# A Mamba block and a routed expert layer on one core: the norm of the block behind moved one step, and the order of the tail on VectorE and GpSimd

## The reference, cut to what matters

```python
def step(h, inp):                     # Mamba: 512 channels, 16 states, over 1024 tokens
    xt, dt_t, B_t, C_t = inp
    A_disc = jnp.exp(A[None, None, :] * dt_t[:, :, None])
    h = A_disc * h + dt_t[:, :, None] * B_t[:, None, :] * xt[:, :, None]
    y_t = jnp.einsum('bed,bd->be', h, C_t) + D * xt
    return (h, y_t)
...
y = jax.nn.silu(y + res)
return y @ W_out.T
...
x = _layernorm(x + mamba(x), axis=-1)                 # (x - m) / sqrt(v + 1e-5)
router_probs = jax.nn.softmax(x @ router_w.T)
expert_weights, expert_idx = jax.lax.top_k(router_probs, 2)
# each of the two experts: gelu(x @ w1.T + b1) @ w2.T + b2, weighted and summed
x = _layernorm(x + moe(x), axis=-1)
```

## Time and profile before

| | us |
|---|---|
| median of 3 runs | 1429.03 (1427.63 to 1429.11) |
| the profiled execution, own time | 1429.47 |
| its span in the profile | 1427.7 |
| PE busy | 1288.1 (90%) |
| DVE busy | 1104.4 (77%) |
| POOL busy | 1052.6 (74%) |
| ACT busy | 993.4 (70%) |
| first scan to last scan (`mamba`'s blocks) | 40.4 to 855.1 |
| mean granted clock of PE | 0.962 of full speed |

### The profile page before, as it was taken

How to read it: one execution, slowest core, us unless ns; L and a number is a source line. 1 busy time by engine, 2 the same in 40 slices (tenths; PEclk the granted TensorE clock), 3 DMA queues, 4 the chain that set the end, 5 groups by cost and what they waited for, 6 DMA issues and landing times. The chain is left out here.

```text
span 1427.7 us, 28835 instructions
## 1 busy us (share of the span) xinstructions
PE 1288.1 (90%) x8807; PEld 1090.3 (76%) x8808; DVE 1104.4 (77%) x1836; ACT 993.4 (70%) x1364; POOL 1052.6 (74%) x920
## 2 busy tenths in 40 slices
PE   6799899999998998998997996499999999999991
PEld 2468687787777787877886885499999999999981
DVE  6879999899899899899898896665665665665554
ACT  6899998999988999988988963334433433433434
POOL 3589798798998989998989997455555555555544
PEclk8799999999999999999999998699999999999995
DMA  8523141132331332331322327424465723522216
GB/s 280 173 79 97 61 122 63 56 120 79 101 108 68 99 103 71 105 104 64 109 82 75 111 85 246 152 42 107 123 160 144 206 41 74 140 41 37 34 20 243
DMA packets 91017, 150.75 MB, mean 106 GB/s; under 512 B 10892, under 2 KB 43276, under 8 KB 90928
## 3 DMA queue, kind: packets, MB, share of 16 engines
q1 hardware_dynamic: 73216, 121.24, 26.4%
q0 software_dynamic: 16704, 27.29, 9.5%
q10 hardware_dynamic: 1008, 1.07, 0.3%
HBM read 100.79 MB, written 48.78 MB: 105 GB/s over the span
## 5 line engine op out<-in xcount | busy, mean ns | idle before, releaser
L1448 POOL TENSOR_TENSOR arena<-arena 128x1024 f32<-128x1024 f32 x252 | 598.5, 2388 | 16.5 <-DVE arena L1107 10.1
L492 PE MATMUL d_ps<-ident,arena 128*128 128x128 f32 x2048 | 320.7, 280 | 44.2 <-DVE arena L1107 36.7
L492 PEld LDWEIGHTS d_ps<-ident,arena 128*128 128x128 f32 x2048 | 240.9, 143 | 150.4 <-DVE arena L1107 73.1
L1107 DVE TENSOR_TENSOR_SCAN arena<-arena,carry,d_ps 128x512 f32<-128x512 f32 x256 | 314.5, 1264 | 28.5 <-PE d_ps L492 21.5
L793 ACT ACTIVATE arena<-u_tok,b_tok 128x512 f32<-128x512 f32 x508 | 324.5, 711 | 6.5 <-PE d_ps L492 5.1
L1107 DVE TENSOR_TENSOR_SCAN arena<-arena,d_ps 128x512 f32<-128x512 f32 x256 | 301.2, 1207 | 30.1 <-PE d_ps L492 19.7
L505 PE MATMUL y_ps<-ident,arena 128*128 128x128 f32 x2048 | 297.3, 274 | 6.8 <-POOL arena L1448 5.5
L1796 ACT ACTIVATE h_t<-ht_ps 128x512 f32<-128x512 f32 x142 | 84.4, 594 | 284.0 <-PE ht_ps L1851 284.0
L807 ACT ACTIVATE arena<-dt,neg_a 128x2048 f32<-128x2048 f32 x127 | 253.1, 1993 | 2.3 <-DVE arena L1107 2.1
L505 PEld LDWEIGHTS y_ps<-ident,arena 128*128 128x128 f32 x2048 | 238.0, 142 | 9.5 <-POOL arena L1448 6.6
L1836 PE MATMUL h_ps<-arena,xg_t 128*128 x852 | 218.1, 405 | 1.3 <-DVE xg_t L1928 1.3
(11 more groups left out here) (230 smaller groups left out, 1552.7 us busy)
## 6 DMA issues: line engine op xcount, KB each, us to landing
arena<-c_rows SPq DMA_DIRECT2D x128, 256.0 KB, 3.3
arena<-weight_parts SPq DMA_DIRECT2D x20, 1024.0 KB, 5.5
weight_parts<-arena SPq DMA_DIRECT2D x64, 256.0 KB, 3.6
xg<-expert_rows POOLq DMA_DIRECT2D x71, 130.0 KB, 2.4
arena<-in_pieces SPq DMA_DIRECT2D x16, 512.0 KB, 8.9
arena<-in_pieces SPq DMA_DIRECT2D x64, 128.0 KB, 3.3
expert_out<-arena SPq DMA_DIRECT2D x1, 4224.0 KB, 15.2
weight_parts<-arena SPq DMA_DIRECT2D x4, 1024.0 KB, 4.6
```

Of the source, the lines that this page charges most:

```text
L492: last = nc.tensor.matmul(d_ps[:, c % 2, j * P:(j + 1) * P], ub[:, g % U_RING, j, c * P:(c + 1) * P], t.ident[:], start=True, stop=True, i ...
L1107: nc.vector.tensor_tensor_scan(h[:, g % H_RING, c, :], decay[:, g % D_RING, c, :], d_ps[:, c % 2, :], 0.0 if i % 2 == 0 else carry[:, n, c ...
L1448: nc.gpsimd.tensor_tensor(h[:, g % H_RING, lo:hi, :], h[:, g % H_RING, lo:hi, :], c_row[:, g % C_RING:g % C_RING + 1, :].broadcast_to([P, ...
```

## The change

Three edits, all of order. No instruction, DMA, buffer or semaphore is added or taken away, and the counts that are waited for stay the same.

1. ACT: `normed()` at the end of step 13 instead of step 14, in blocks 1 to 6. It now comes behind `ut_out(0)` and before `ut_out(1)`. In block 7 it stays at step 12.
2. DVE, in the tail: `copy_group(2)` is ahead of `router_place()` instead of behind it and behind a low part. `own_low(0)` and `own_low(1)` stand together behind the last `norm_group`, ahead of `router_pick(r)`. `own_low(2)`, `(3)` and `(4)`, which stood in the tail, move behind `tables()`, ahead of the seven that were there, so that ten stand there.
3. POOL, in the tail: before, the order was send 0, root 0, send 1, root 1, send 2, root 2, send 3, root 3, sends 4 to 7 (of block 6). Now it is send 0, root 0, send 1, root 1, root 2, root 3, sends 2 to 7.

```diff
--- before.py
+++ after.py
@@ -1074,7 +1074,7 @@
                         xp_out(e, 1)
                     if front and n == 13:
                         ut_out(0)
-                    if back and n == (12 if i == BLOCKS - 1 else 14):
+                    if back and n == (12 if i == BLOCKS - 1 else 13):
                         normed()
             iterations(act, step)
             store_tails(act, range(EXPERTS // 2, EXPERTS))
@@ -1279,9 +1279,8 @@
                     router_sum()
                     router_invert()
                     router_rank()
+                    copy_group(2)
                     router_place()
-                    own_low(0)
-                    copy_group(2)
                     add_group(0)
                     copy_group(3)
                     add_group(1)
@@ -1291,11 +1290,9 @@
                     add_group(3)
                     norm_group(2)
                     norm_group(3)
+                    own_low(0)
                     own_low(1)
-                    own_low(2)
                     router_pick(r)
-                    own_low(3)
-                    own_low(4)
                     router_sum(r)
                     router_invert(r)
                     router_rank(r)
@@ -1426,7 +1423,7 @@
             nc.vector.memset(member[:, TT, :], 0.0)
             iterations(dve, step)
             tables()
-            for m in range(5, W_RING * W_LOADS):
+            for m in range(2, W_RING * W_LOADS):
                 own_low(m)
 
         @block.gpsimd
@@ -1569,10 +1566,11 @@
                                                         (tail_i, [[REGION, EXPERTS]], 0, 0), (pad_i, [[0, 1]], TOKENS, 1)):
                         nc.gpsimd.iota(out, pattern=pattern, base=base, channel_multiplier=channel).then_inc(made, 1)
                     send_rows(p, 0)
-                    for j in range(TT):
+                    rstd_group(0)
+                    send_rows(p, 1)
+                    for j in range(1, TT):
                         rstd_group(j)
-                        send_rows(p, j + 1)
-                    for m in range(TT + 1, TT * TOPK):
+                    for m in range(2, TT * TOPK):
                         send_rows(p, m)
                     router_member(r)
                     router_shift(r)
```

## The result

The changed kernel takes 1415.34 us (median of 4 runs, 1412.16 to 1415.51) against 1429.07 us for the kernel before in the same session. The ratio is 0.9897, with a 95% interval of 0.9878 to 0.9916. The profiled execution is the fastest of the four: 1412.16 us, with a span of 1410.5.

The account below looks back on a forecast made before the run. Bound: across block ends ACT, DVE and PE wait in turn, while ACT work could fill ACT's earlier idle time. Five blocks at 1.45 us, plus 0 for the sixth and the tail, give 7.25: 1429.03 becomes 1421.8, range 1418.0 to 1426.0.

Parts of the forecast that it names:

- Part 1: Blocks 1 to 6: ACT's norm a step sooner, in ACT's idle time; 7.25 us sooner, bounds 4.7 and 9.2.
- the sum of 7.25: Block ends: five blocks at 1.45 us each plus 0 for the sixth block.
- Odd blocks: Ends of blocks 1, 3 and 5: norm fits ACT's idle 2.21; 1.45 us gained each, bounds 1.2 and 1.84.
- the decay's wait: Block after an odd block: DVE's 2.12 us wait for ACT's decay stays, both being ahead by the same.
- from there PE ran to the end of the next block's first transposes in 2.55: Odd block's end: PE's transposes start 1.2 us sooner, then take 2.55 as before, ending at 245.35.
- Rival A: Block ends: ACT is all of the chain, five blocks give 1.84 us each, 9.2, so 1419.8; chance 0.17.
- Even blocks: Ends of blocks 2 and 4: 1.45 us each, bounds 1.0 and 1.6; POOL's products leave 1.57 of slack.
- Block 6: Its end: gain 0; DVE scans delayed up to 1.0 us in step 14 lie under a 3.31 wait; otherwise 0.9 paid.
- Part 2: Tail reordered on POOL and DVE: last norm 1.95 us sooner, net 0; bounds 0.9 sooner and 1.2 later.
- a sign of being wrong: Tail: the prediction would be wrong if POOL's sends or the first x part moved by more than 1 us.
- one such: Tail: one of six sends held 0.9 us by the second low part; `router_member(r)` at about 885.8 instead of 885.27.
- the loads of rows: Tail: POOL's first loads now run beside low parts; one took 0.61 us there before, so no cost taken.

Follow-up runs that it names:

- experiment 1: Norm moved to step 13 in odd blocks alone, old tail, against the kernel before: 1424.12 against 1429.14 us.
- experiment 2: Norm moved to step 13 in blocks 2, 4 and 6 alone, old tail, against the kernel before: 1421.89 us, ratio 0.9952.
- experiment 3: Kernel before, norm and tail unmoved, DVE's dt-xc multiplies asked for at other scans in odd blocks: 1427.35 against 1429.14 us.
- experiment 4: Changed kernel with DVE's first dt-xc multiply one scan earlier in blocks 3 and 5: 1418.21 against 1414.58 us for the changed kernel.
- Experiment 6: Kernel before with two of the norm's four instructions in step 13, two in step 14, blocks 1 to 6: 1422.82 against 1428.59 us.
- experiment 8: Changed kernel with the norm back in step 14, so the new tail alone, against the kernel before: 1428.22 against 1429.14 us.

## Why the prediction was wrong

**The step that failed: Part 1 takes the middle of a block as fixed.** The text says "all of the PE-full middle starts 1.45 sooner", and the sum of 7.25 has no term for it. It rests on one middle, that of block 2, where PE has no gap. In block 3 PE was busy 23.62 of 25 us. In blocks 3 and 5 the middle held 2.4 and 2.1 us in which DVE's multiply waited for POOL, and the change took them away by shifting DVE against POOL at the even blocks' ends: by 1.4 us in block 3, and by 1.8 in block 5, where the scans come 8.2 sooner and POOL's last products of block 4 6.4. Experiments 1, 2, 3 and 4 show it from four sides: without the shift there is no gain, with it there is, by moving the multiply the gain comes without the norm, and by moving it back it goes. This is 4.5 of the 6.5 us missed; the ends were 0.95 too small in the sum and the tail 0.9.

**Odd blocks: mechanism right, size too small.** The norm went into ACT's idle time as said, the tap came 1.85 sooner (forecast 1.8), the decay's wait stayed. 1.45 was forecast, 1.7 to 1.8 measured. The mis-sized term is "from there PE ran to the end of the next block's first transposes in 2.55": it takes 245.65 - 243.31 = 2.34 now that DVE's scans are sooner; and the transposes start 1.35 sooner, not 1.2. Experiment 6 adds that of a shift of 1.03 on ACT 0.97 to 0.98 comes through, so for the odd blocks Rival A, that the chain is ACT's, was the better account.

**Even blocks: right.** 1.35 and 1.65 against 1.45 (bounds 1.0 and 1.6), with POOL as the bound that was named: the sums now start 0.10 after the products. Block 4's 1.65 lies a hair above its bound. That the norms overrun ACT's idle time does not show in these numbers. But this is also where the shift comes from, since DVE gains there and POOL does not. **Block 6: right.** In step 14 DVE falls back by 0.66, less than the 1.0 allowed for, and block 7 gives it back.

**Part 2, the tail: 0 forecast, 0.8 to 0.9 by medians, 1.4 in the profiles.** Neither median is clear of the noise. The first x part came 1.4 sooner against the last scan, more than the 1 us that the prediction had named as a sign of being wrong. The last norm came 1.9 sooner, as forecast, and the six sends started where they were said to. The wrong term is the "one such" send that is held (0.9) and with it the half us of delay. The second send started at 865.77, as the first low part ended and 0.01 us ahead of the second; it kept its 0.97. In all six profiles with both new orders it did, but nothing in the change was made to bring that about: the order was decided by a hair. The low parts after the tables cost nothing, and the loads of rows beside them took 0.6, as the prediction had it.

**Profiles and medians.** The profiled execution of before lost 1.26 us to the low clock in block 7, and the one of after had the best mean clock of its four (0.968 against 0.963 to 0.964), so the profiles differ by 17.2 us and the medians by 13.7. The parts add up to the latter, 8.2 + 4.5 + 0.9 = 13.6, with the tail's 0.9 as the least certain of them.

**How the hold works.** Over the 14 profiles with this multiply, in all 123 cases where it was asked for more than 0.2 us before the end of a POOL tensor_tensor under way, its length was that remainder plus 1.08 us (1.077 to 1.088). So it did not go on before POOL's instruction was over. When DVE started just ahead, POOL's instruction was the longer one, by about 1.0 (1.73 instead of 0.73 in block 3). The Trainium skill (SBUF — State Buffer, Who interferes with whom) states it as an exclusive lock for a whole instruction between a DVE instruction with two SBUF inputs and a GpSimd one that reads SBUF; the trace agrees but for 0.15 us, since the multiply takes 1.23 alone and 1.08 from the product's end. The prediction weighed this rule for the tail only, where it spoke of loads, and did not put it to the block's middle.

## What to carry to other kernels

When a change moves one engine against another, look at every pair of instructions on the two that exclude each other, over all stages, not only at the chain that you shorten: here holds of up to 1.7 us came and went with shifts of 1 to 1.5 us. Two queries find it cheaply: the spread of one line's lengths (here 1.22 to 2.96 us for one and the same instruction), and the windows of a stage in every block rather than in one. And a place that is free in one trace is only free as long as nothing ahead of it is moved: in experiments 3, 4 and 6 a multiply met a product that the trace in hand had not shown in its way.

## What the runs showed of the hardware that I had not expected

- POOL's indirect sends are held by a DVE instruction with two SBUF inputs too: in the 60 cases of the 14 profiles in which a send of rows started inside such a subtraction or product (128x1024), more than 0.2 us before its end, it took 1.37 to 1.97 us instead of 0.96 and ended 0.83 to 0.84 us after it, and it took 0.97 when it started just ahead of one. The Trainium skill (SBUF — State Buffer, Who interferes with whom) reports that a tensor_tensor did not stall a DMA in a probe, and infers that it leaves descriptor generation alone. For the instruction by which POOL issues an indirect send the measurement says otherwise; whether it is the reading of the offsets that waits, no run here shows. The plain loads of rows (0.6) were not held.
- The order of arrival decides who pays: DVE in blocks 3 and 5 before, POOL after.
- TensorE's granted clock fell to 0.50 of full speed in block 7 of before, after PE waits of 0.94, 0.52, 0.52 and 0.61 us, and stayed at 1.00 in the changed kernel's first profile after the same four waits. After a wait of 2.29 us in the tail it fell in experiment 8 and stayed at 1.00 in the changed kernel. These two falls cost 1.26 and 1.69 us.
